# An attention and mixture-of-experts block on one core: another opening order, 16-bit halves in the feed-forward layers, a norm moved to VectorE

## The reference

```
x = x + layernorm(attention(layernorm(x)))
x = x + layernorm(ffn(layernorm(x)))

attention: q, k, v = x wq^T, x wk^T, x wv^T      (16 heads of 64)
           q, k = rotary(q), rotary(k)
           p = softmax(causal(q k^T / 8));  out = (p v) wo^T
ffn:       h = x lin0_w + lin0_b
           h = silu(h swi1_w1 + b) * (h swi1_w2 + b)
           scores = softmax(h gate^T), best 4 of 8 experts, renormalised
           h = sum of experts (silu(h w1) * (h w3)) w2, weighted by scores, + a shared expert twice as wide
           h = h lin1_w + lin1_b
           h = silu(h swi2_w1 + b) * (h swi2_w2 + b)
```

## Time and profile before

| | before |
|---|---|
| median of 3 runs | 1192.29 us (1190.64 to 1192.48) |
| the profiled execution's own time | 1189.41 us |
| its span, first to last instruction | 1187.5 us |
| mean granted TensorE clock | 0.978 |
| TensorE matmul busy | 93% of the span |
| VectorE, ScalarE, GpSimd busy | 81%, 81%, 80% |

### The profile page before, as it was taken

One profiled execution on the slowest core, in us unless ns is written; L12 is line 12 of the kernel. 1 busy time (PEld: TensorE's weight loads), 2 busy tenths in 40 slices (PEclk: granted clock), 3 DMA queues, 4 the chain that ended last, 5 costly groups with the idle time before them and its releaser, 6 DMA issues. The chain is left out here.

```text
span 1187.5 us, 36496 instructions
## 1 busy us (share of the span) xinstructions
PE 1110.2 (93%) x14311; PEld 800.0 (67%) x14311; DVE 959.2 (81%) x2195; ACT 956.4 (81%) x2205; POOL 951.1 (80%) x1064
## 2 busy tenths in 40 slices
PE   4689999999999999999999999999998788999996
PEld 1256777777777777777777777777776555666663
DVE  7789787978879797979788797979895359767977
ACT  7767989889797979798897979798887767756574
POOL 3569899999999999999999999999784567434663
PEclk9689999999999999999999999999998999999999
DMA  6761525252533425152515345252611000000011
GB/s 194 167 151 38 144 49 132 73 126 57 143 82 99 106 75 145 39 142 73 134 48 143 79 103 121 61 145 54 163 32 39 15 23 2 1 1 1 2 37 36
DMA packets 50475, 97.24 MB, mean 82 GB/s; under 512 B 8512, under 2 KB 25152, under 8 KB 46272
## 3 DMA queue, kind: packets, MB, share of 16 engines
q1 hardware_dynamic: 50304, 94.92, 31.6%
HBM read 58.47 MB, written 34.60 MB: 78 GB/s over the span
## 5 line engine op out<-in xcount | busy, mean ns | idle before, releaser
L916 POOL TENSOR_TENSOR Plo<-P,Phi 128x512 f16<-128x512 f32 (+3 forms) x634 | 531.6, 866 | 68.1 <-ACT P L566 66.4
L563 ACT ACTIVATE Phi<-psS 128x512 f16<-128x512 f32 (+3 forms) x768 | 394.6, 514 | 125.3 <-PE psS L413 74.1
L566 ACT ACTIVATE P<-psS 128x512 f32<-128x512 f32 (+3 forms) x634 | 313.8, 496 | 0.0
L435 PE MATMUL psO<-V,Plo 128*128 128x65 f16 x2304 | 289.2, 194 | 0.0
L431 PE MATMUL psO<-V,Phi 128*128 128x65 f16 x2304 | 288.6, 193 | 0.6 <-POOL Plo L916 0.6
L433 PE MATMUL psO<-V,Phi 128*128 128x64 f16 x2304 | 287.5, 192 | 0.0
L402 PE MATMUL psS<-Q,K 128*128 128x512 f16 (+3 forms) x768 | 252.8, 329 | 17.6 <-DVE Plo L742 13.0
L431 PEld LDWEIGHTS psO<-V,Phi 128*128 128x128 f16 x2304 | 216.1, 98 | 42.5 <-POOL Plo L916 1.4
L791 DVE TENSOR_REDUCE pmax<-psX 128x1 f32<-128x512 f32 x384 | 242.1, 681 | 0.2
L433 PEld LDWEIGHTS psO<-V,Phi 128*128 128x128 f16 x2304 | 214.9, 97 | 31.2 <-issue 1.1
L435 PEld LDWEIGHTS psO<-V,Plo 128*128 128x128 f16 x2304 | 214.4, 97 | 0.0
(11 more groups left out here) (215 smaller groups left out, 2500.7 us busy)
## 6 DMA issues: line engine op xcount, KB each, us to landing
k_way<-HL SPq DMA_DIRECT2D x64, 256.0 KB, 3.9
K<-k_way SPq DMA_DIRECT2D x32, 512.0 KB, 8.4
q_way<-HL SPq DMA_DIRECT2D x60, 256.0 KB, 3.7
Q<-q_way SPq DMA_DIRECT2D x15, 1024.0 KB, 11.8
K<-k_way SPq DMA_DIRECT2D x32, 256.0 KB, 4.3
Q<-q_way SPq DMA_DIRECT2D x30, 256.0 KB, 5.3
out<-y SPq DMA_DIRECT2D x8, 256.0 KB, 2.2
y<-in_x SPq DMA_DIRECT2D x3, 512.0 KB, 10.4
```

The source lines that it names most:

```text
L435: mm = nc.tensor.matmul(O, M.Plo[:, U % NP_, k * P:(k + 1) * P], V[:, HD:2 * HD + 1], start=False, stop=j == t, skip_group_check=True)
L563: nc.scalar.activation(M.Phi[:, U % NP_, 0:w], X, ACT.Exp, scale=SCALE)
L566: nc.scalar.activation(full, X, ACT.Exp, scale=SCALE).then_inc(S.exp_done, 1)
L916: nc.gpsimd.tensor_tensor(M.Plo[:, U % NP_, 0:w], M.P32[:, U % NP_, 0:w], M.Phi[:, U % NP_, 0:w], ALU.subtract).then_inc(S.lo_pool, 1)
```

## The change

The opening's tables are written anew; `pace` lets several `mx` banks share a step; all V items of the first group now stand before slot 0; the second group's `mx` steps are written out. In slot 0 all low halves but one go to GpSimd, and in the last group all of its first head's. The second norm of the first eight tiles goes from ScalarE to VectorE. In the feed-forward part `first` of blocks 2 to 7 and `lin1` and `last` of blocks 0 to 6 are made of 16-bit halves. `V_LAG` is 0, and `EXP_TABLE` and `M.spare` are set and used nowhere.

```diff
-QK_EARLY = ((2, 3, 4, 5, 6, 7, 8, 9), (0, 1, 2, 3, 16, 17, 18, 19))
-V_FIRST = ((-1, 4), (-1, 5), (0, 1), (0, 3))
-MX_FIRST_GROUP = ((-1, 7), (-1, 20), (0, 0), (0, 8))
-JOIN_FIRST = ((-1, 15), (-1, 28), (0, 8), (0, 16))
-MT_FIRST = ((-1, 17), (0, 1), (0, 11), (0, 19))
-MX_SECOND, JOIN_SECOND, MT_SECOND = (13, 41), 42, 44
+QK_EARLY = ((2, 3, 4, 5, 6, 7, 8, 9), (0, 1, 4, 4, 15, 17, 27, 28))
+V_FIRST = ((-1, 4), (-1, 10), (-1, 40), (-1, 41))
+MX_FIRST_GROUP = ((-1, 18, 1), (-1, 29, 3), (0, 2, 1), (0, 6, 1))
+JOIN_FIRST = ((-1, 28), (-1, 39), (0, 11), (0, 21))
+MT_FIRST = ((-1, 29), (0, 5), (0, 20), (0, 29))
+MX_SECOND = (13, 13, 14, 15, 15, 16, 17, 17, 18, 19, 19, 20, 21, 24, 24, 24, 25, 26,
+             26, 26, 27, 27, 28, 29, 30, 30, 31, 31, 32, 32, 33, 34, 34, 34, 35, 36)
+JOIN_SECOND, MT_SECOND = 39, 42
+QK_SECOND, V_SECOND = (1, 2, 9, 10, 15, 17, 23, 27), (2, 12, 35, 42)
+LO_SECOND = (34,)
+V_LAG = 0
+EXP_TABLE = (-1, 29)
-FAR_AT = {..., (-1, 20): (12, 13), (-1, 22): (14, 15)}
+FAR_AT = {..., (-1, 27): (12,), (-1, 5): (13,), (-1, 32): (14,), (-1, 0): (15,)}
-X_SQUARE = {(-1, 5): (1, 2), (-1, 17): (3,)}
-X_ROOT, X_RECIPROCAL = (-1, 19), (0, 6)
+X_SQUARE = {(-1, 10): (1, 2), (-1, 12): (3,)}
+X_ROOT, X_RECIPROCAL = (-1, 28), (-1, 32)
-AHEAD = (...) + ... + ((LAST, 38, 39),)
-ROOTS_AT = ((LAST - 1, 14, 28), (LAST, 29, 36))
+AHEAD = (...) + ... + ((LAST, 38, 46),)
+ROOTS_AT = ((LAST - 1, 14, 28), (LAST, 29, 34))
...
 def lo_on_pool(U):
     if U >= SU * LAST:
-        return U % NU not in LO_END
+        return U < SU * LAST + NU or U % NU not in LO_END
     if U >= SU * LAST - LO_FREE:
         return True
-    return U % NU not in LO_DVE
+    return U % NU not in LO_DVE if U >= SU else U not in LO_SECOND
...
-                if s == LAST and 0 <= u - NORMAL_AT < TT:
-                    ...
-                    nc.scalar.activation(M.sin[:, t * D:(t + 1) * D], M.y[:, t, :], ACT.Identity, scale=M.rstd[:, t:t + 1],
-                                         bias=M.std[:, t:t + 1])
...
                 dve.wait_ge(S.roots_done, 2)
-                nc.vector.scalar_tensor_tensor(out=M.std[:, 0:TT], in0=M.mv[:, 0:TT, 0], scalar=-1.0, ...
-                yield
+                for t in range(TT):
+                    nc.vector.tensor_scalar(x_tile(t), M.y[:, t, :], M.mv[:, t, 0:1], M.rstd[:, t:t + 1], ALU.subtract,
+                                            ALU.mult)
+                    yield
...
-                        for _ in range(i + 1):
+                        for _ in range(1 + 2 * i):
                             next(roots[i], None)
...
+    def halves(x):
+        kind, k = x
+        return k >= WHOLE_FIRST if kind in ("lin0", "first") else k < blocks - 1
...
                 elif kind == "lin1":
-                    pe.wait_ge(S.moe_out, k + 1)
-                    mm = nc.tensor.matmul(X, M.wd[:, 3, :], R.mT[:, k % 2, :], start=True, stop=True)
+                    if halves(x):
+                        pe.wait_ge(S.m_lo, k + 1)
+                        for q, (wi, xi) in enumerate([(0, 0), (0, 1), (1, 0)]):
+                            mm = nc.tensor.matmul(X, R.w5[:, wi, 2, :], R.mTs[:, k % 2, xi, :], start=q == 0, stop=q == 2)
+                    else:
+                        ...
...
+                if halves(x):
+                    if kind == "first":
+                        pe.wait_ge(S.w5_lo, 1)
+                        pe.wait_ge(S.h0_lo, k + 1 - WHOLE_FIRST)
+                        to = R.h0s
+                    else:
+                        pe.wait_ge(S.h3_lo, k + 1)
+                        to = R.h3s
+                    for j, bank in enumerate((R.psG, R.psU)):
+                        for q, (wi, xi) in enumerate([(0, 0), (0, 1), (1, 0)]):
+                            mm = nc.tensor.matmul(bank[:, n % 2, :], R.w5[:, wi, w - 1 + j, :], to[:, k % 2, xi, :], ...
...
                 if n == SPLIT_LAST:
                     split(2)
+                    nc.scalar.copy(R.w5[:, 0], M.wd[:, 1:6, :]).then_inc(S.w5_hi, 1)
...
+                elif kind == "lin0" and halves(x):
+                    dve.wait_ge(S.lin0_out, k + 1)
+                    nc.vector.scalar_tensor_tensor(out=R.h0s[:, k % 2, 1, :], in0=Z(x), scalar=M.bias[:, 0:1],
+                                                   in1=R.h0s[:, k % 2, 0, :], op0=ALU.add,
+                                                   op1=ALU.subtract).then_inc(S.h0_lo, 1)
+                elif kind == "moe" and halves(x):
+                    dve.wait_ge(S.moe_out, k + 1)
+                    nc.vector.tensor_tensor(R.mTs[:, k % 2, 1, :], Z(x), R.mTs[:, k % 2, 0, :],
+                                            ALU.subtract).then_inc(S.m_lo, 1)
+                elif kind == "lin1" and halves(x):
+                    ...
...
             for k in range(3):
                 weight_low(k)
+            pool.wait_ge(S.w5_hi, 1)
+            nc.gpsimd.tensor_tensor(R.w5[:, 1], M.wd[:, 1:6, :], R.w5[:, 0], ALU.subtract).then_inc(S.w5_lo, 1)
```

More of the change, by code:

```diff
@@ L135, in plan @@
             for r in range(8):
-                put(s, QK_STEPS[r] if s >= 0 else QK_EARLY[s + 2][r], ("qk", r // 4, r // 2 % 2, r % 2))
+                put(s, (QK_STEPS if s else QK_SECOND)[r] if s >= 0 else QK_EARLY[s + 2][r], ("qk", r // 4, r // 2 % 2, r % 2))
         if s >= -1 and s + 1 <= LAST:
@@ L141, in plan @@
                 else:
-                    put(s, V_STEPS[tp], ("v", tp))
+                    put(s, (V_STEPS if s else V_SECOND)[tp], ("v", tp))
             for h in range(GH):
@@ L145, in plan @@
                     if s < 0:
-                        slot, u = MX_FIRST_GROUP[h]
-                        at.setdefault((slot, u + k), []).append((s, "mx", h, k))
+                        slot, u, pace = MX_FIRST_GROUP[h]
+                        at.setdefault((slot, u + k // pace), []).append((s, "mx", h, k))
                     else:
                         i = h * len(MAXB) + k
-                        first, last = MX_SECOND
-                        put(s, MX_STEPS[i] if s > 0 else first + i * (last - first) // (GH * len(MAXB) - 1),
-                            ("mx", h, k))
+                        put(s, MX_STEPS[i] if s > 0 else MX_SECOND[i], ("mx", h, k))
             if s < 0:
@@ L368, in attention_block @@
     dve_at, act_at = late(DVE_LAG), late(ACT_LAG)
+    for (s, u), items in list(dve_at.items()):
+        for item in [x for x in items if V_LAG and s <= 0 and x[1] == "v"]:
+            items.remove(item)
+            dve_at.setdefault((s, u + V_LAG), []).append(item)
     def rope_items(s, u, early, later):
@@ L1345, in z_taken @@
         elif kind == "moe":
-            eng.wait_ge(S.moe_out, k + 1)
+            if halves(x):
+                eng.wait_ge(S.m_lo, k + 1)
+            else:
+                eng.wait_ge(S.moe_out, k + 1)
         elif kind == "lin1":
-            eng.wait_ge(S.lin1_out, k + 1)
+            if halves(x):
+                eng.wait_ge(S.h3_lo, k + 1)
+            else:
+                eng.wait_ge(S.lin1_out, k + 1)
         else:
@@ L1389, in side @@
                 elif kind == "lin1":
-                    pe.wait_ge(S.moe_out, k + 1)
-                    mm = nc.tensor.matmul(X, M.wd[:, 3, :], R.mT[:, k % 2, :], start=True, stop=True)
+                    if halves(x):
+                        pe.wait_ge(S.m_lo, k + 1)
+                        for q, (wi, xi) in enumerate([(0, 0), (0, 1), (1, 0)]):
+                            mm = nc.tensor.matmul(X, R.w5[:, wi, 2, :], R.mTs[:, k % 2, xi, :], start=q == 0, stop=q == 2)
+                    else:
+                        pe.wait_ge(S.moe_out, k + 1)
+                        mm = nc.tensor.matmul(X, M.wd[:, 3, :], R.mT[:], start=True, stop=True)
                 else:
@@ L1482, in side @@
                         z_wait(act, ("lin1", k - 2))
-                    nc.scalar.copy(R.mT[:, k % 2, :], Z(x)).then_inc(S.moe_out, 1)
+                    nc.scalar.copy(R.mTs[:, k % 2, 0, :] if halves(x) else R.mT[:], Z(x)).then_inc(S.moe_out, 1)
                 elif kind == "lin1":
```

53 lines of the change are left out of this document (35 added, 18 removed).

## The result

The changed kernel took 1182.08 us (median of 5 runs, 1180.91 to 1182.27) beside 1191.11 for the kernel before in the same session (5 runs, 1187.95 to 1192.48): ratio 0.9925, 95% interval 0.9911 to 0.9940. That is 9.0 us faster, faster by more than 0.2%. The forecast was 17.7 us, 1174.6; the time lies in the range of 1167 to 1183, near its upper end. So the sign and the range were right and the size was twice too large, and the question is which terms of the sum did not come.

The account below looks back on a forecast made before the run. TensorE, busy 93% of the span, was taken as the bound, so gains come only where it waits. Gains of 6.5 + 2.5 + 2.8 + 5.9 = 17.7 us off 1189.41 gave 1171.7, as a median 1174.6; range 1167 to 1183.

Parts of the forecast that it names:

- Opening, 6.5 us: Up to the second group: VectorE sheds work to GpSimd, so the group starts at 124.4, not 130.9; ends -9.5 and -1.
- the rival in which it takes VectorE's place: Slot 0: GpSimd becomes the pace, holds the rotations too, and the opening brings only 1 us; 1180; chance 0.09.
- Last group, first head, 2.5 us: With all twelve low halves on GpSimd, the head takes 11.4 us instead of 13.90; ends 0 and -3.4.
- I count 0.9 us of it after the slack of the steps: Last group's first head: of up to 4.8 us delay of VectorE's sums beside GpSimd, 0.9 us counts.
- Last head, 2.8 us: Last group's last head: ScalarE loses eight activations, so it takes 10.2 us instead of 13.00; ends -3.5 and -1.4.
- what is left is 8.7: Last head: ScalarE's 12.82 us busy less eight activations of 4.1 us leaves 8.7 us.
- The rival's mechanism: Last head: each of eight normal tiles on VectorE waits out a 512-wide low half, 11.5 us; 1180.5; chance 0.05.
- Feed-forward, 5.9 us: Feed-forward part: 16-bit halves save 7.9 us on TensorE, less waits and copy, net 5.9; ends -7.5 and -3.
- each is due a full place before its reader, while copy and low half take 1.3: Feed-forward from 1000 to 1100: VectorE's low halves have a place of 1.97 us, needing 1.3, before they are read.
- a sign of being wrong: Feed-forward: a stall by a low half of `moe` or `lin1` was listed among observations that would show the prediction wrong.
- VectorE's low halves eat the gain, 1180.5: Feed-forward: VectorE fills up with 14 us of low halves against 5.9 won, so the part brings nothing; chance 0.05.
- The copy of the weights, 0.7 us: Feed-forward start: ScalarE's copy of five weights, 640 columns, stands on the chain and adds 0.7 us.

Follow-up runs that it names:

- run 9: Kernel before with the opening's part of the change alone (order of first two groups, slot 0's low halves to GpSimd): 1183.41 us, ratio 0.9936.
- Runs 2 and 3: Changed kernel with, in turn, the last group's first-head low halves shared with VectorE again (1179.87 us), and most sums moved to step 10 on (1177.0 us).
- Run 6: Changed kernel with the second norm of the first eight tiles put back on ScalarE: 1183.89 us, ratio 0.9943.
- run 7: Changed kernel with 16-bit halves only in `lin0` and `first`; `moe`, `lin1` and `last` in float32 as before: 1182.98 us, ratio 0.9935.
- run 4: Changed kernel with ScalarE's copy of the five weights put behind the next chunk's high half: 1181.2 us, ratio 0.9924.
- run 1: Changed kernel with every feed-forward edit undone, opening and last group kept: 1184.19 us, ratio 0.9944.
- run 12: Repeat, in the last session, of the changed kernel with every feed-forward edit undone: 1183.07 us, ratio 0.9937.

## Why the prediction was right in sign and wrong in size

- **Opening, 6.5 us: right.** The gain is 6.84 at the second group, run 9 has 6.5 there and keeps it to the last group. VectorE was the pace, GpSimd took the work (58.14 of 59.31 us), TensorE's weight loads waited for its low halves only 1.4 us in all, and the rival in which it takes VectorE's place did not come.
- **Last group, first head, 2.5 us: wrong, -1.8.** The step that failed is "I count 0.9 us of it after the slack of the steps". The bound that I worked out from the earlier trace rows for the sums was 4.8 us; the wait that came was 4.68. My price of 0.88 a sum was the mean of a stretch in which one sum got in ahead of the low halves and three stood beside narrow ones; with the head's low halves, six of them 512 wide, it was 1.03. That is a small part of it. The large one is that nothing of the bound was hidden: the scaling stands straight behind the sums. And having seen that a wait of 2.75 us halved the clock, I did not carry that to my own new wait: the ends of 0 and -3.4 left out a loss altogether. Runs 2 and 3 show both halves: the head at 13.02 with the old sharing, at 9.41 with the sums moved, better than the 10.5 that I had (1.1 us of it comes back in the second head).
- **Last head, 2.8 us: 1.74, mis-sized.** Run 6 confirms what the move is worth to 0.1 us. The term that was off is "what is left is 8.7": ScalarE's busy time fell from 12.82 to 10.13 us, by 2.69 and not by 4.1, since 4.1 is the sum of eight durations that overlap the instructions behind them (one stands at 929.95 for 0.49 us, and the next starts at 930.35). With 1.10 us of idle time the head's exponentials take 11.23 us, not 10.2. VectorE's eight cost 0.73 us each (5.6 us in all), inside the 0.28 to 0.88 allowed. The rival's mechanism was there in part: two of them took 0.33 with GpSimd idle, six stood beside a low half for 0.47 to 1.20. But that is half of its 11.5 us, and VectorE, busy 8.77 of 11.23, had room for it.
- **Feed-forward, 5.9 us: 0.9 in the pair of profiles, 2.5 over all profiles, 2.4 by ratios.** The saving per pair was as in the earlier trace rows. The step that failed is "each is due a full place before its reader, while copy and low half take 1.3": in three of the four waits the full place is there, but the copy or the low half is not next in its engine's queue. In the two longest the low half stands behind VectorE's other work and starts 1.3 us after the high half is done. From chunk 8 on my terms give 6.6 us and 1.96 came. The four waits for `mTs` lost 2.1 us of chunk pitch, and `first` in halves brought nothing at all (run 7) though I had 1.9 us for its four pairs outside the start; that is 4.0 of the 4.6 that are missing. A stall by a low half of `moe` is also what I had named as a sign of being wrong. I had this as a rival (VectorE's low halves eat the gain, 1180.5) with a chance of 0.05. It came half true, and its time, 1180.5, is nearer than my own. It was not want of VectorE's time that did it (84.41 of 98 us), but its order.
- **The copy of the weights, 0.7 us: right in size.** Taking it away is worth 0.6 to 0.8 us where the clock falls alike (run 4). ScalarE's timeline of the kernel after has it at 0.72, between the cast L1574 and the high half L1549 that the earlier trace rows chain to TensorE, whose wait behind them is 2.29 us there and 1.66 in the kernel before.

```profile
949.80 1.25 ACT L1574 CAST ws<-Q 128x1280 f16<-128x1280 f32 x1
950.95 0.72 ACT L1595 CAST w<-wd 128x640 f16<-128x640 f32 x1
951.58 0.62 ACT L1549 CAST h1s<-h1T 128x512 f16<-128x512 f32 x1
```

- **From execution to median.** The profiled pair differs by 7.1 us and the medians by 9.0: the execution that I summed against is 1.7 us under the median of before in the session of the result, the profiled one of after 0.2 over its own. The good start above would account for it, but no second profile of the kernel before is there to show it. So about 2 of the 9 us that were measured are not of the sum at all, and with one term right, one at two thirds, one under half and one lost, that the time still lies in the range owes something to luck.

## What to carry to other kernels

Before work moves to GpSimd, list what VectorE does in the same microseconds, pair its instructions with GpSimd's one for one, and see what stands behind them in its queue: here ten low halves beside eight sums cost more than the wait that they removed, and moving the sums out of the way gave 5.2 us in the two heads and 3 to 4 of the whole. Do not take durations off a stage where they overlap; take the difference of busy times. For a split operand, count what the low half's engine has ahead of it at that very spot. And take a stage whose clock falls from execution to execution from several profiles: a single one can hold its best case.

## What the runs showed that I had not expected

- The same eight sums in the same order took 6.51 us in one execution (run 1) and 8.15 in another of the same kernel (run 12), and the head took 11.4 and 15.7 us. The pairing of sums with low halves shows where the 1.6 us lie; what put VectorE 0.4 to 0.5 us ahead in that one execution is open.
- TensorE's granted clock fell after a wait of 4.7 us (to 0.50, 1.2 GHz, for some 4 us) and stayed at 1.00 after the one of 2.5 in run 1, while in runs 2 and 9 it fell after 2.8. In the start of the feed-forward part it fell in 13 of 14 profiles, at different places; the kernel before in its one exception did the same work there.
- VectorE and GpSimd took turns one for one, instruction by instruction, whenever sums met low halves, so that a sum of 0.34 us took 0.51 to 1.24 by the width of the low half beside it. The mean of eight, 0.88 or 1.03, is a mean over widths. A TENSOR_SCALAR of 128x128 took 0.33 alone and up to 1.20 beside one.
